# A gated cross-attention block with a feed-forward: batch 2 alone first and batch 3 alone last, a table load one copy later, VectorE's early work in another order

## The reference

```
q = c Wq^T + bq ; k = c Wk^T + bk ; A = softmax(q k^T)        # 256 x 256, no scaling
x2 = x + tanh(g_xattn) * layernorm(x) A^T
h  = e4m3(layernorm(x2))
a  = gelu_tanh(h @ e4m3(Wg[0])) * (h @ e4m3(Wg[1]))           # 1024 hidden, bf16 results
out = x2 + tanh(g_ffn) * (e4m3(a) @ e4m3(Wl))
```

## Time and profile before

| | |
|---|---|
| Median of 3 runs | 49.64 us |
| Profiled execution | 49.62 us, span 47.8 us |
| TensorE busy | 42.3 us |
| VectorE busy | 33.6 us |
| ScalarE busy | 27.9 us |
| GpSimd busy | 22.2 us |
| Instructions | 861 |

### The profile page before, as it was taken

The page is one execution under the profiler, slowest core; times in us unless marked ns, Lnnn a source line. Parts: engine busy times, 40 slices in busy tenths (PEclk is TensorE's granted clock), DMA queues, the critical chain, the costliest instruction groups (busy, mean ns, idle before and its releaser), DMA issues.

```text
span 47.8 us, 861 instructions
## 1 busy us (share of the span) xinstructions
PE 42.3 (88%) x246; PEld 28.6 (60%) x246; DVE 33.6 (70%) x107; ACT 27.9 (58%) x63; POOL 22.2 (46%) x48
## 2 busy tenths in 40 slices
PE   3998999999999789999989999999999999998000
PEld 1317788877878377865226655565645888884000
DVE  0101629856999998839999999187669977999600
ACT  0901866997889904084549876964448495363000
POOL 3200495484988897810049249980000069700500
PEclk9999999999999999999999999999999999999999
DMA  0499999999999972000000000000000002450092
GB/s 0 70 369 382 341 385 375 368 123 109 105 104 60 81 71 19 14 0 0 0 7 0 0 0 0 0 0 0 0 7 0 0 14 86 168 185 0 7 338 101
DMA packets 3461, 4.65 MB, mean 97 GB/s; under 512 B 384, under 2 KB 2176, under 8 KB 3456
## 3 DMA queue, kind: packets, MB, share of 16 engines
q1 hardware_dynamic: 2304, 3.48, 20.7%
q0 software_dynamic: 864, 0.79, 18.7%
q10 hardware_dynamic: 288, 0.33, 1.9%
HBM read 5.90 MB, written 1.05 MB: 145 GB/s over the span
## 4 chain that ended last, share of the span: by engine, by line
PE 58%; DVE 13%; ACT 9%; DMA 6%; issue 5%; DVEq 2%; POOL 1%; POOLq 0%
PE bank L702 11%; PE bank L631 9%; PE bank L683 8%; PE bank L677 8%; PE bank L596 7%; DMA par<-params_ctxT 6%; PE bank L580 5%; DVE ap L495 4%; PE bank L588 4%; PE bank L603 3%; ACT L404 3%; DVE x L466 3%; DVE st L471 2%; ACT attnT L358 2%; ACT e L352 2%
## 5 line engine op out<-in xcount | busy, mean ns | idle before, releaser
L378 ACT ACTIVATE gl<-bank 128x512 bf16<-128x512 f32 (+1 forms) x20 | 10.2, 510 | 6.4 <-PE bank L677 5.9
L495 DVE SCALAR_TENSOR_TENSOR ap<-bank,gl 128x512 f16<-128x512 f32 (+1 forms) x20 | 11.6, 581 | 3.3 <-PE bank L683 1.8
L683 PE MATMUL bank<-xq,wg 128*128 128x512 fp8e4 (+1 forms) x40 | 10.2, 337 | 0.2 <-DVE ap L495 0.2
L677 PE MATMUL bank<-xq,wg 128*128 128x512 fp8e4 (+1 forms) x40 | 10.2, 337 | 0.0
L702 PE MATMUL bank<-wl,aq 128*128 128x256 fp8e4 x64 | 9.6, 273 | 0.0
L631 PE MATMUL bank<-attnT,xT_sb 128*128 128x256 f32 x32 | 8.5, 393 | 0.5 <-ACT attnT L358 0.5
L702 PEld LDWEIGHTS bank<-wl,aq 128*128 128x128 f16 x64 | 6.2, 98 | 2.4 <-DVE aq L504 0.2
L631 PEld LDWEIGHTS bank<-attnT,xT_sb 128*128 128x128 f32 x32 | 5.4, 190 | 1.9 <-ACT attnT L358 1.5
L683 PEld LDWEIGHTS bank<-xq,wg 128*128 128x128 fp8e4 x40 | 3.6, 98 | 3.9 <-DVE ap L495 1.4
L504 DVE TENSOR_SCALAR aq<-ap 128x512 uint16<-128x512 uint16 (+1 forms) x20 | 5.9, 298 | 0.0
L285 POOL TENSOR_TENSOR r<-ve,neg_half 128x2 f32<-128x2 f32 x4 | 3.2, 788 | 5.9 <-DVE ve L478 5.9
(11 more groups left out here) (50 smaller groups left out, 55.6 us busy)
## 6 DMA issues: line engine op xcount, KB each, us to landing
x_sb<-x SPq DMA_DIRECT2D x4, 256.0 KB, 4.9
xT_sb<-xT SPq DMA_DIRECT2D x4, 256.0 KB, 5.5
out<-yo SPq DMA_DIRECT2D x5, 128.0 KB, 1.7
wg<-w_gating POOLq DMA_DIRECT2D x4, 128.0 KB, 7.6
par<-params_ctxT SPq DMA_DIRECT2D x1, 256.0 KB, 3.4
wl<-w_linear POOLq DMA_DIRECT2D x2, 128.0 KB, 6.1
out<-yo SPq DMA_DIRECT2D x1, 256.0 KB, 2.2
par<-params_ctxT SPq DMA_DIRECT2D x1, 194.0 KB, 3.0
```

The costliest lines, as they stand in the source:

```text
L378: nc.scalar.activation(gl[:, s % 2, toks], gate_b[s % 2][:, toks], ACT.Gelu_apprx_tanh).then_inc(gelu_ready, 1)
L495: nc.vector.scalar_tensor_tensor(ap[:, s % NAP, toks], up_b[s % 2][:, toks], ACT_SCALE, gl[:, s % 2, toks], ALU.mult, ALU.mult).then_inc(p ...
L677: mm = nc.tensor.matmul(gate_b[s % 2][:, toks], wg8[:, c, k, 0, o:o + P], xq[:, g, k, toks], start=(k == 0), stop=(k == KC - 1))
L683: mm = nc.tensor.matmul(up_b[s % 2][:, toks], wg8[:, c, k, 1, o:o + P], xq[:, g, k, toks], start=(k == 0), stop=(k == KC - 1))
```

## The change

The list of steps is rewritten: group 0 as before; of group 1, tiles 0 to 3 of batch 2 alone (steps 8 to 11), tiles 4 to 7 of both batches (12 to 15), tiles 0 to 3 of batch 3 alone (16 to 19). Accumulation of a batch starts and stops with that batch's own first and last step. ffn2 of step s - 2 stands behind step s in steps 2 to 10, that of 9 behind 12, of 10 behind 14, and from 16 on s - 5. ScalarE normalises batch 2 after gelu 4 (before: 3) and batch 3 after gelu 7 (5); the transposes stand between gate and up of steps 5 and 9, instead of behind steps 4 and 6. The table load goes behind the third `attn_out`. VectorE adds batch 2 whole and takes one statistics pass of it before `xq_half`; each round follows its own product at once; the statistics of batch 3 are spread over steps 2 and 3.

```diff
-    STEPS = [divmod(n, HT) + (0, GB) for n in range(G * HT - SPLIT)]
-    STEPS += [(G - 1, j, i, i + 1) for i in range(GB) for j in range(HT - SPLIT, HT)]
+    STEPS = [(0, j, 0, GB) for j in range(HT)]
+    STEPS += [(1, j, 0, 1) for j in range(SPLIT)]
+    STEPS += [(1, j, 0, GB) for j in range(SPLIT, HT)]
+    STEPS += [(1, j, 1, GB) for j in range(SPLIT)]
-    FFN2_AT = {s: (s - 3,) for s in range(3, 10)}
-    FFN2_AT |= {s: (s - 5,) for s in range(12, S)}
+    FFN2_AT = {s: (s - 2,) for s in range(2, 11)}
+    FFN2_AT |= {12: (9,), 14: (10,)} | {s: (s - 5,) for s in range(16, S)}
-    NORM2_AFTER = (3, 5)
-    X_AFTER = (4, 6)
+    NORM2_AFTER = (4, 7)
+    X_BESIDE = (5, 9)
...
+            attn_out(2)
             nc.scalar.activation(table[:, :], tg[:, 0:1], ACT.Gelu_apprx_tanh)
-            attn_out(2)
             attn_out(3)
...
-            add_attention(2, [0])
+            add_attention(2)
+            stats2(2, 0)
             xq_half()
-            add_attention(2, [1])
             add_attention(3)
-            stats2(2, 0)
             stats2(2, 1)
             dve.wait_ge(yscale_ready, 1)
             for s in range(S):
-                if s == S - 1:
-                    round_product(s - 1)
                 product(s)
-                if 1 <= s < S - 1:
-                    round_product(s - 1)
+                round_product(s)
                 if s == 0:
                     moments2(2)
                 if s == 2:
-                    stats2(B - 1, 0)
-                    stats2(B - 1, 1)
+                    stats2(3, 0)
                 if s == 3:
-                    moments2(B - 1)
-            round_product(S - 1)
+                    stats2(3, 1)
+                if s == 4:
+                    moments2(3)
...
+                for b in range(B):
+                    if s == first_step(b):
+                        pe.wait_ge(xq_ready, b + 1)
...
                 mm.then_inc(gate_done, 1)
+                if s in X_BESIDE:
+                    turn_x2(2 + X_BESIDE.index(s))
                 if s >= 2:
                     pe.wait_ge(prod_ready, s - 1)
...
-                                          start=(j == 0 and t == 0), stop=(j == HT - 1), skip_group_check=True)
+                                          start=(s == first_step(b) and t == 0), stop=(s == last_step(b)),
+                                          skip_group_check=True)
```

More of the change, by code:

```diff
@@ L201, in flamingo_block, with steps_of, first_step @@
         s_out = sem("s_out")
+        def steps_of(b):
+            return [s for s, (g, _, i0, i1) in enumerate(STEPS) if GB * g + i0 <= b < GB * g + i1]
+        def first_step(b):
+            return min(steps_of(b))
         def last_step(b):
-            return max(s for s, (g, _, i0, i1) in enumerate(STEPS) if GB * g + i0 <= b < GB * g + i1)
+            return max(steps_of(b))
         block = ctx.enter_context(nc.Block())
@@ L414, in _ @@
                     norm2(3)
-                if s == X_AFTER[0]:
+                if s == X_BESIDE[0]:
                     xq_out(2)
-                if s == X_AFTER[1]:
+                if s == X_BESIDE[1]:
                     xq_out(3)
@@ L460, in xq_half, with add_attention @@
                                       saturate=False).then_inc(xq_half_ready, 1)
-            def add_attention(b, ts=range(LT)):
+            def add_attention(b):
                 dve.wait_ge(pv_done, b + 1)
                 dve.wait_ge(s1_ready, b // GB + 1)
-                for t in ts:
+                for t in range(LT):
                     nc.vector.scalar_tensor_tensor(x2[:, b, t], halves(pv_b[b % 2])[:, t], s1[:, b, t:t + 1], x_sb[:, b, t],
@@ L663, in ffn1 @@
                 toks = slice(i0 * L, i1 * L)
-                if j == 0:
-                    pe.wait_ge(xq_ready, GB * (g + 1))
+                for b in range(B):
+                    if s == first_step(b):
+                        pe.wait_ge(xq_ready, b + 1)
                 if s == 0:
@@ L695, in ffn2 @@
                     pe.wait_ge(xq_ready, 2)
-                if s == HT:
-                    pe.wait_ge(xq_ready, B)
                 for i, t in ((i, t) for i in range(i0, i1) for t in range(LT)):
                     m = (i * LT + t) * P
+                    b = GB * g + i
+                    if g == 1 and t == 0 and s == first_step(b):
+                        pe.wait_ge(xq_ready, b + 1)
                     mm = nc.tensor.matmul(halves(y_b[g][i])[:, t], aq[:, s % NAQ, m:m + P], wl8[:, j],
-                                          start=(j == 0 and t == 0), stop=(j == HT - 1), skip_group_check=True)
+                                          start=(s == first_step(b) and t == 0), stop=(s == last_step(b)),
+                                          skip_group_check=True)
                 mm.then_inc(ffn2_done, 1)
@@ L736, in _ @@
                     ffn2(done)
[L737 to L740, removed]
             for s in range(S - 5, S):
```

## The result

The changed kernel took 50.15 us (median of 4 runs, 49.91 to 50.51) against 49.58 us; the ratio is 1.0152 (95% interval 1.0083 to 1.0222). It is slower, and 50.15 lies above the stated range, which ended at 50.05. Run again later beside other kernels, the ratio was 1.0067 (1.0008 to 1.0127). The ratios leave out executions that took over 1.5% more than the fastest of the same kernel; the medians do not. The profiled execution took 49.97 us, span 48.2, against 49.62 and 47.8.

What follows compares the result with a forecast made beforehand. TensorE, 88% busy, was the bound, so only its waits count. From 49.62 us: head -0.18, old waits -0.90, step 5 +0.53, up(16) and up(17) +0.62, tail -0.16, giving 49.53, stated 49.55; forecast 49.3 to 49.7, wider range 49.1 to 50.05.

Steps and rivals of the forecast that it cites:

- VectorE's rounds and GpSimd's additions: Steps 13 to 17: round 14 starts near GpSimd's third addition; wait at up(17) 0.62 us if let through, 1.10 if held.
- the rival called slower: VectorE at gate(17): addition starts first and holds round 14, 0.48 us more at up(17), total 50.0; chance 0.25.
- The layout: Feed-forward steps timed from profile spacings, claimed good to about 0.1 us; forecast's last VectorE addition ends at 45.04.
- the row nearest in distance: Earlier trace's round at 39.37, 0.05 before GpSimd's second addition, took 0.22 us; cited for round 14 being let through.
- Head: Attention part: table load behind ScalarE's third copy lets batch 3's transposes start earlier, gaining 0.18 us, bounds 0 and 0.29.
- Waits at up(2), up(3), before batch 3's transposes and at up(12): Feed-forward: TensorE's old waits of 0.41, 0.15, 0.22 and 0.12 us go, 0.90 in all.
- Wait at step 5: Between gate and up, TensorE newly waits 0.53 us for ScalarE's normalisations of batch 2; bounds 0.4 to 0.65.
- Steps 13 to 17 without held rounds: ScalarE's two scale-outs delay gelu 15 and product 15, so TensorE waits 0.55 us by up(17), 0.12 already at up(16).
- Round 13: VectorE's round of step 13 is held by GpSimd's first output addition, moving product 14 by 0.24 us, product 15 by 0.07.
- Tail: From up(17) to VectorE's last addition 4.91 us; last DMA issue 0.02 to 0.25 behind; gives 0.16 us back.
- the fourth copy: Attention part, ScalarE: not delayed by the 1.28 us table load; rival with drain: 0.5 late, 50.1 us, chance 0.03.

Runs made afterwards that it cites:

- the other branch forced: Changed kernel with GpSimd's third output addition waiting until step 14's round is done; ratio 0.9976, first gate matmul to VectorE's last addition 23.62 us.
- the run with the rounds behind: Changed kernel with the rounds of steps 13, 14 and 15 each issued behind the next step's product; ratio to the kernel before 1.0046.
- the run without additions: Changed kernel without GpSimd's four output additions of batches 0 and 1, their residual left out of the output; ratio to the kernel before 0.9937.
- the early part: Kernel before with only the table load behind the third copy and VectorE's new order up to the first product; ratio 0.9825.

## Why the prediction was wrong

*The failed step* is the choice in "VectorE's rounds and GpSimd's additions": "I take 0.62, the smaller, because the two starts lie within 0.06 of each other". Round 14 was held, in both profiles of the changed kernel; the waits at up(16) and up(17) were 0.23 + 0.59 = 0.82 as the profile counts them (behind the pipeline's end; by slots, as the prediction counts, 0.39 + 0.75 = 1.14, where it has 1.10). That is the rival called slower, to which I gave 0.25 and 50.0 us, and the profile took 49.97. The layout for that branch has B at 45.52 - 21.38 = 24.14, and 24.11 was measured. With the other branch forced, B was 23.62, where the layout has 45.04 - 21.38 = 23.66. So the mechanism and both prices were right, and the choice between them was wrong.

What I had called the row nearest in distance, 39.37 in the earlier trace rows, was no evidence for it: that round started 0.04 us before the addition, and my own layout had the addition first, by 0.06. The trace of the kernel before has no round that started less than 0.11 us behind a GpSimd instruction. The other traces have some, and the closest were let through. In the changed kernel, at step 6, a round started 0.02 us behind one of the shifts (`shift_residual`, line 287) and took its 0.30 us, while the shift took 0.59 instead of 0.48:

```profile
31.08 0.59 POOL L287 TENSOR_SCALAR xr<-x,nms 128x256 f32<-128x256 f32 x1
31.10 0.30 DVE L511 TENSOR_SCALAR aq<-ap 128x512 uint16<-128x512 uint16 x1
```

Over all profiles, rounds up to 0.035 us behind such a start went through; the nearest that was held, round 14 of the run with the rounds behind, came 0.065 behind its addition. A calculated 0.06 therefore lay beside the turning point, with an error of 0.1 on it. The order of the layout came true, at 0.09; one case can't say how far such an order may be trusted, but nothing in the trace of before favoured the other one.

*The range* ended 0.05 above that rival's own sum, and I had allowed nothing for the spread of the runs. The median of four runs was 0.18 above the profiled one, which alone would have stayed inside the range. In the repeat of the changed kernel the profiled execution took 0.37 us more than the first (50.34), and its first gate came 0.37 later with the same B. That the same lies behind the 0.18 is likely, but these executions have no profile. So it was luck on which side of 50.05 the median fell, and not luck that it missed the forecast by half a microsecond.

Point by point, in the order of the sum. Head: 0.18 predicted, A moved by 0.19. Waits at up(2), up(3), before batch 3's transposes and at up(12): all gone but for 0.01 us, as predicted. Wait at step 5: 0.53 predicted, 0.53 in the profile, 0.54 by experiment. Steps 13 to 17 without held rounds: 0.55 predicted, 0.10 + 0.40 = 0.50 by slots in the run without additions; taking them out gave back 0.65 of B, where the layout has 0.55 (1.10 less 0.55); product 15 came 0.05 later than laid out with them and 0.06 earlier without. Round 13: 0.41 longer than free, 0.43 measured. Tail: ScalarE's scaled copy sets VectorE's last three additions, as laid out, and from up(17) to their end it took 4.82 (4.91 predicted); the last issue came 0.03 behind VectorE's last addition, at the near end of the 0.02 to 0.25 given. GpSimd's half started 0.10 behind the copy, so the queue was free again in time.

The table's load took 1.28 us and its activation started 0.01 behind; the fourth copy was not delayed, as the row of before had it. The Trainium skill ("ScalarE: Activation LUTs", What ACT_TABLE_LOAD costs) adds a drain of about 1.38 us to a load; it does not show here, and the measured 0.01 stands.

By the Trainium skill ("SBUF — State Buffer", SBUF: two separate sides), of VectorE and GpSimd the one that starts first holds the shared port pair for its whole instruction. For the output additions the traces agree: the held rounds of 0.72, 0.78 and 0.81 us each ended 0.15 behind an addition that had started before them, and rounds 13 and 14 took 0.29 without additions. Three things in the traces are finer than the rule. A round that starts in the last 0.13 us or so of a GpSimd record is not held, as the one at 39.37 in the earlier trace rows, where the first addition's record reached to 39.45. A round up to 0.035 us behind the start goes through. And GpSimd's instruction for the reciprocal root, on two elements per partition, held nothing, though its record was as long as an addition's. In the kernel before the round of step 0 lay inside it:

```profile
24.52 0.82 POOL L285 TENSOR_TENSOR r<-ve,neg_half 128x2 f32<-128x2 f32 x1 [4.03 <-DVE ve L478]
...
25.02 0.28 DVE L504 TENSOR_SCALAR aq<-ap 128x512 uint16<-128x512 uint16 x1
```

## What to carry to other kernels

Count where an instruction can be held by another engine, and ask what stands behind it in its own list: the same collision cost nothing behind the product and half a microsecond in front of it. When a layout by hand gives two starts within its own error, the case is open, with a known price at either side: look in the trace for pairs at the same distance and in the same order, and let the range hold both ends with the spread of the runs added. A change of many parts can hide a good one: here the early part was worth 0.7 us by the distances, and two numbers of the later part (where ScalarE normalises and where it scales out) took that and more; both were found by asking of each wait in the profile which single position makes it.

## What the runs showed of the hardware

A round of 128x512 16-bit values takes 0.28 to 0.30 us alone and up to 0.81 when one of GpSimd's 128x256 additions of two float tensors started before it; the products, which read PSUM and one tensor of SBUF, took 0.68 to 0.69 beside the same additions. A held round ends 0.15 us behind the end of the addition's record (0.08 for a half-size one, which takes 0.22 alone), so the loss is nearly all that is left of the addition. It was held 0.065 us behind the start of an addition. GpSimd's shifts of 0.48 us hold too: the round of step 2 took 0.53 to 0.55 us in the changed kernel and in all runs made from it, where nothing waited for it.

The feed-forward and all behind it repeated to 0.01 us between the two profiles of the changed kernel, while over the profiles of all kernels the start of the attention moves by 1.3 us. Comparing distances inside the profile resolved 0.1 us, where twelve timed runs left an interval of half a per cent to either side.
